# Four graph layers for 128 small graphs on one core: new instruction orders, the residual constant in two pairs, and unsplit transposed weights read out by ScalarE

## The chip, the core and the metric

The kernel runs on one core of a Trainium2 chip. It has TensorE (PE; its weight loads are a track of their own, PEld), VectorE (DVE), ScalarE (ACT), GpSimd (POOL), the queue that issues most transfers (SP) and 16 DMA engines. The metric is device time in microseconds of one launch.

## The reference, cut to what matters

```python
x = layernorm(x + gcn(x, adj) )          # h = x@W + b; adj@h / row sum of adj
x = layernorm(x + linear_att(x, adj))    # softmax over nodes of q.(adj@(k*mask)) / 16, times v
x = layernorm(x + mha(x, adj))           # 8 heads, scores * (adj + adj), softmax, Wo
x = layernorm(x + hyper(x, adj))         # D^-1 H B^-1 H^T(.)W^T + b twice, relu and layernorm between
```

x is 128 graphs x 128 nodes x 256, adj is 128 x 128 x 128, the weights are 256 x 256 to 256 x 512, all in float32. The last layer's result is y + x, and a constant part of y that depends only on the node (its count times beta@W2, plus the bias b2, halved) is added to the residual beforehand: this is the residual constant, c3.

## The kernel before

The graphs are worked on in 32 groups of G = 4. The work of a group is cut into stages, and a step is one stage of one graph (or of the whole group), such as `h1.2`. Matrix products of stages marked by six or twelve passes are made from operands split in a high and a low part (`rows3`, L516); ACT writes the high part out of PSUM and DVE the low part (`copy_out` L716, `low` L1041). Each layernorm runs DVE (statistics, L1026 and L1031), POOL (root, L884 to L889), ACT (normalise, L724).

**Who orders the work.** Nothing is scheduled at run time. Every engine walks a list of steps written out by hand, and waits on semaphores in that order. There are three lists for each engine: FIRST_TEXT (group 0's first half, and all preparation of weights), ORDER_TEXT (one round, walked 31 times: once, and then in a loop of 30), LAST_TEXT (second half of the last group). In a round, a step with + belongs to the next group, one without to the present group, so each round has the early stages (at, ax, h0, x1t, amx, xg, wt, pb, v1, x2t, q, k, mp, sc, z, exp) of one group among the late ones (pt, cx, wo, tx, h1, mn, y) of the group before. On the PE list the number behind the colon is the PSUM bank (of 8) that the step fills; pt, sc0 and sc1 take two banks from that number. A step waits until those who read the bank's earlier content are done (`early`, L471 on).

**Steps that the change and the prediction touch.**

- `c3` (POOL, `c3_`, L956 to L963): the residual constant of all four graphs in two instructions of 128x1024 (L959 multiply, L962 add). `x3b` (L969) adds it to the normalised x3 of one graph; `y` on DVE needs that.
- `wm` (POOL, L925): w times mask, 128x4; it waits for the four xg reads of DVE (L1064). `wt` (PE, L540) transposes it, then follow wmax and wnorm (DVE), wexp (ACT), and `pb` (PE, L544). In the POOL order of a round, wm stands right behind c3.0; in the PE order wt stands behind tx.1 (L610).
- `pt` (PE, L589): eight transposes of one graph's attention; `pt` on ACT (L792) copies two banks to pT in one instruction of 128x1024; `cx` (PE, L597) reads pT. cx.0 is the first PE step of a round.
- `exp0`, `exp1` (ACT, L785): four heads each, eight instructions; `mp` (PE L569, ACT L716): 128x130; `hb` (POOL, L930) is needed by mp.
- `turn` (PE, L633): the 20 transpositions of weights in FIRST. `turnhi`/`turnlo` (ACT L802, DVE L1161) read out those of v, q, k and w1 in two parts. The twelve others (mask, q and k of layer 1, the row vectors, o and w2) stay unsplit, and DVE copies them (`turn_lo`, L1158). `scale` (DVE, L1179) multiplies w2 by gamma once all of w2 is read out, `hi_w2`/`lo_w2` (ACT L817, DVE L1185) split it.
- `ACT_LOADS` (L869): ACT issues the loads of L1's Wqk (512 KB), L0's W and L1's Wv (256 KB each) before its first step. All other transfers are issued by SP (L392 to L429).

Of the kernel before, what the change touches and what calls it, by code (L numbers as in the profile page):

```python
# [17 lines left out]
P = 128  # L18
G = 4
HEADS = 8  # L20
RG = 4
# [32 lines left out]
        ln2_norm.0 ax.3+ ln0_norm.0+ v2.3 tx.0 exp0.3 ln0_norm.1+ x1t.0+ exp1.3 x1t.1+ amx.0+ ln0_norm.2+
        pt.2 x1t.2+ amx.1+ ln0_norm.3+ cx.2 amx.2+ ln2_norm.1 x1t.3+ hbc.0+ amx.3+ relu.0 pt.3 cx.3 tx.1
        wexp.0+ ln3_norm.0 ln2_norm.2 ln2_norm.3 tx.2 ln1_norm.0+ mn.0 ln1_norm.1+ relu.1 ln1_norm.2+ tx.3
        x2t.0+ ln1_norm.3+ x2t.1+ x2t.2+ x2t.3+ relu.2 relu.3 ln3_norm.1 q0.0+ k1.0+ q1.0+ ln3_norm.2 k0.0+
# [9 lines left out]
        wmax.0+ tx_lo.1 ln2_aggr.2 wnorm.0+ wo.3 ln2_stats.3 pcol.0+ ln2_aggr.3 v1.0+ v1.1+ ln1_stats.0+
        ln1_aggr.0+ v1.2+ ln1_stats.1+ ln1_stats.2+ ln1_aggr.1+ ln1_aggr.2+ v1.3+ tx_lo.2 ln1_stats.3+ h1.1
        ln1_aggr.3+ mn_lo.0 ln3_stats.1 tx_lo.3 x2t_lo.0+ x2t_lo.1+ x2t_lo.2+ x2t_lo.3+ h1.2 h1.3 ln3_aggr.1
        y.0 ln3_stats.2 ln3_stats.3 ln3_aggr.2 ln3_aggr.3 ln4_stats.0 ln4_aggr.0 mn_lo.1 z0.0+ z1.0+  # L70
        zmax0.0+ mn_lo.2 y.1 ln4_stats.1 zmax1.0+ ln4_aggr.1 z0.1+ mn_lo.3 zmax0.1+ zrcp.0+ z1.1+ y.2
# [32 lines left out]
        hT.0+ ax_lo.0+ turnlo.0+ asum.0+ turnlo.1+ hT.1+ hT.2+ hT.3+ turnlo.2+ lo_w0.0+ ax_lo.1+ turnlo.3+
        turnlo.4+ h0.0+ ln0_stats.0+ ax_lo.2+ ln0_aggr.0+ h0.1+ ln0_stats.1+ ax_lo.3+ ln0_aggr.1+ h0.2+
        ln0_stats.2+ gramlo.0+ ln0_aggr.2+ h0.3+ gramlo.1+ ln0_stats.3+ x1t_lo.0+ ln0_aggr.3+ x1t_lo.1+
        turnlo.5+ turnlo.6+ xg.0+ x1t_lo.2+ xg.1+ x1t_lo.3+ lo_wv1.0+ xg.2+ xg.3+ turnlo.7+ wmax.0+ wnorm.0+
        pcol.0+ v1.0+ ln1_stats.0+ v1.1+ ln1_aggr.0+ v1.2+ ln1_stats.1+ turnlo.8+ ln1_aggr.1+ ln1_stats.2+
# [1146 lines left out]
```

## Time and profile before

| | us |
|---|---|
| median of 3 runs (1754.32 to 1756.01) | 1755.94 |
| the profiled execution | 1754.82 |
| its span, first to last instruction | 1753.1 |
| PE busy in the span | 1725.9 |
| DVE, ACT, POOL busy | 1457.4, 1445.5, 1381.3 |
| granted TensorE clock, mean | 1.0 |

The profiled execution's own time is 1.7 us above its span. Engines' busy times are unions of the recorded instructions; matmuls overlap in the records, so for PE the distance from one start to the next says more than a duration. A row of a timeline is: start, length, engine, line, operation, output<-inputs, shapes, count, and in brackets the idle time before it with its releaser.

### The profile page before, as it was taken

How to read it: one execution, taken by the hardware profiler on the slowest of the kernel's cores; microseconds unless marked ns; L12 is line 12 of the kernel's file. 1: busy time of each engine (PE TensorE's matmuls, PEld its weight loads, DVE VectorE, ACT ScalarE, POOL GpSimd, SP SyncE). 2: the span in 40 equal slices, each digit the busy share in tenths (PEclk: the TensorE clock that was granted, in tenths of full speed). 3: DMA queues.
4: the chain of work that ended last, by engine and by line, in shares of the span. 5: the costliest groups of instructions: out<-in, count | busy, mean ns of one | idle time of the engine just before them, and what ended most of it. 6: DMA issues, size and time to landing. Idle time of an engine off the chain costs nothing. (4 is left out here: it accounts for less than half of the span.)

```text
span 1753.1 us, 52062 instructions
## 1 busy us (share of the span) xinstructions
PE 1725.9 (98%) x15358; PEld 1557.1 (89%) x15358; DVE 1457.4 (83%) x4038; ACT 1445.5 (82%) x4463; POOL 1381.3 (79%) x2825
## 2 busy tenths in 40 slices
PE   8999999999999999999999999999999999999997
PEld 6889888999889898889998998988899989989886
DVE  7988888888888888888888888888888888888886
ACT  4888888888888888888888888888888888888886
POOL 4777778787788877787877888777878778887776
PEclk9999999999999999999999999999999999999999
DMA  4111101111001111011110011110111100111000
GB/s 132 31 44 43 33 16 34 42 42 37 19 27 42 42 42 33 16 34 42 42 37 20 27 42 42 42 33 16 34 42 42 36 21 27 42 42 42 27 6 22
DMA packets 93590, 62.94 MB, mean 36 GB/s; under 512 B 8430, under 2 KB 92924, under 8 KB 93564
## 3 DMA queue, kind: packets, MB, share of 16 engines
q1 hardware_dynamic: 92748, 61.58, 11.7%
q10 hardware_dynamic: 816, 1.05, 0.2%
q8 instruction: 12, 0.20, 0.0%
q14 instruction: 14, 0.11, 0.0%
HBM read 45.82 MB, written 16.78 MB: 36 GB/s over the span
## 5 line engine op out<-in xcount | busy, mean ns | idle before, releaser
L785 ACT ACTIVATE z<-z,z_max 128x128 f32<-128x128 f32 x1024 | 399.8, 398 | 5.0 <-DVE z_max L1125 3.7
L886 POOL TENSOR_TENSOR ln_rs<-ln_ve,minus_half 128x1 f32<-128x1 f32 x640 | 352.6, 551 | 50.1
L889 POOL TENSOR_SCALAR ln_nm<-ln_mv,ln_rs 128x1 f32<-128x1 f32 x640 | 170.6, 267 | 110.1 <-POOL ln_rs L886 110.0
L884 POOL TENSOR_TENSOR ln_ve<-ln_mv,eps_col 128x1 f32<-128x1 f32 x640 | 122.7, 192 | 163.1 <-DVE ln_mv L1031 162.8
L906 POOL TENSOR_TENSOR z<-z,z_rcp 128x1024 f32<-128x1024 f32 x128 | 243.1, 1899 | 8.7 <-DVE z_rcp L1132 5.5
L516 PE MATMUL ps<-w2T,mnT 128*128 128x256 f32 x1536 | 209.0, 284 | 0.0
L516 PE MATMUL ps<-w1T,txT 128*128 128x512 f32 x768 | 204.5, 403 | 0.2 <-DVE txT L1041 0.2
L785 ACT ACTIVATION_READ_ACCUMULATOR z<-z,z_max 128x1 f32 x1024 | 200.0, 195 | 0.0
L516 PEld LDWEIGHTS ps<-w2T,mnT 128*128 128x128 f32 x1536 | 188.1, 188 | 4.2 <-DVE mnT L1041 0.4
L1041 DVE TENSOR_TENSOR mnT<-ps,mnT 128x512 fp32r<-128x512 f32 x128 | 86.7, 678 | 111.5 <-ACT mnT L716 111.5
L1125 DVE TENSOR_REDUCE z_max<-z 128x4 f32<-128x512 f32 x256 | 170.2, 675 | 0.1
L1114 DVE SCALAR_TENSOR_TENSOR z<-ps,a_hold 128x512 f32<-128x512 f32 x256 | 166.7, 682 | 0.7 <-PE ps L580 0.4
L516 PEld LDWEIGHTS ps<-w1T,txT 128*128 128x128 f32 x768 | 135.1, 189 | 22.3 <-DVE txT L1041 0.4
L724 ACT ACTIVATE h<-h,ln_nm,ln_rs 128x512 f32<-128x512 f32 x128 | 104.4, 816 | 43.9 <-POOL ln_nm L889 40.4
L621 PE MATMUL ps<-mp,h 128*128 128x128 f32 x1024 | 138.2, 278 | 0.3 <-ACT h L724 0.3
L792 ACT COPY pT<-ps 128x1024 f32<-128x1024 f32 x128 | 129.4, 1011 | 10.7 <-PE ps L589 10.7
L589 PE MATMUL ps<-ident,z 128*128 128x128 f32 x1024 | 134.8, 275 | 0.9 <-POOL z L906 0.8
L1031 DVE BATCH_NORM_AGGREGATE ln_mv<-ln_st 128x2 f32<-128x6 f32 x640 | 112.7, 176 | 27.6
L621 PEld LDWEIGHTS ps<-mp,h 128*128 128x128 f32 x1024 | 126.8, 191 | 6.6 <-ACT h L724 0.5
L516 PE MATMUL ps<-gram,x1T 128*128 128x256 f32 x768 | 126.5, 300 | 0.0
L516 PE MATMUL ps<-w,axT 128*128 128x256 f32 x768 | 126.4, 301 | 0.0
L724 ACT ACTIVATE x<-x2c,ln_nm,ln_rs 128x256 f32<-128x256 f32 x128 | 78.4, 613 | 54.0 <-POOL ln_nm L889 54.0
(154 smaller groups left out, 4912.4 us busy)
## 6 DMA issues: line engine op xcount, KB each, us to landing
x_in<-in_x_dram SPq DMA_DIRECT2D x128, 128.0 KB, 2.1
a_hold<-in_adj_dram SPq DMA_DIRECT2D x128, 128.0 KB, 2.2
out_dram<-y_out SPq DMA_DIRECT2D x128, 128.0 KB, 1.7
a_in<-in_adj_dram SPq DMA_DIRECT2D x128, 64.0 KB, 1.9
h<-in_L_gnn_W_dram SPq DMA_DIRECT2D x2, 512.0 KB, 7.1
x<-in_L_gnn_Wqk_dram ACTq DMA_DIRECT2D x1, 512.0 KB, 3.9
y_out<-in_L_gnn_W_dram ACTq DMA_DIRECT2D x1, 256.0 KB, 4.5
y_out<-in_L_gnn_Wv_dram ACTq DMA_DIRECT2D x1, 256.0 KB, 5.1
```

The source lines that it names most:

```text
L516: m = pe.matmul(o, left(i, c), right(j, c), start=(k == 0), stop=(k == len(passes) - 1))
L589: m = pe.transpose(ps[:, b + h // 4, (h % 4) * P:(h % 4 + 1) * P], z[:, g % 2, h, :], ident[:, :])
L621: m = pe.matmul(o[:, c * P:(c + 1) * P], h1[:, g, c * P:(c + 1) * P], mp[:, g, 0:P], start=True, stop=True)
L724: act.activation(dst(g), src(g), ACT.Identity, bias=nm[n][:, g:g + 1], scale=rs[n][:, g:g + 1]).then_inc(norm_made[n], 1)
L785: m = act.activation(z[:, g % 2, h, :], z[:, g % 2, h, :], ACT.Exp, bias=z_max[:, g % 2, h:h + 1], accum_out=z_sum[:, g % 2, h:h + 1])
L792: act.copy(pT[:, g % 2, :, :].rearrange("p (b h) n -> p b (h n)", b=2), ps[:, b:b + 2, :]).then_inc(read["pt"], 1)
L884: pool.tensor_tensor(ve[n][:, g:g + 1], mv[n][:, g, 1:2], (eps4_col if n == "ln4" else eps_col)[:, :], ALU.add).then_inc(eps_made[n], 1)
L886: pool.tensor_tensor(rs[n][:, g:g + 1], ve[n][:, g:g + 1], minus_half[:, :], ALU.pow).then_inc(root_made[n], 1)
L889: pool.tensor_scalar(nm[n][:, g:g + 1], mv[n][:, g, 0:1], rs[n][:, g:g + 1], -1.0, ALU.mult, ALU.mult).then_inc(shift_made[n], 1)
L906: pool.tensor_tensor(zg, zg, z_rcp[:, g % 2, :].unsqueeze(2).to_broadcast([P, HEADS, P]), ALU.mult)\
L1114: dve.scalar_tensor_tensor(out=z[:, g % 2, hs, :].rearrange("p (r c) n -> p r (c n)", r=RG // 2), in0=ps[:, b:b + RG // 2, 0:C * P], scala ...
L1125: dve.tensor_reduce(z_max[:, g % 2, hs], z[:, g % 2, hs, :], AX.X, ALU.max, negate=True)\
```

## The change

Three things: (1) c3 is made for two graphs at a time (c3.0, c3.1), with semaphore counts to match, and x3b.g waits for its pair alone. (2) The twelve unsplit transposed blocks are copied out of PSUM by ACT (`turncp`, semaphore `whole_read`) and no longer by DVE; ACT issues only the load of w0 first, then does its first step (at.0), then issues qk1 and wv1. (3) All the orders and bank numbers are new. Of the round, mp.2 and mp.3 move to the start of the next round on PE, v2.2 to the end of the round before, x2c.3 (POOL), z1.2 (DVE), and the load lh.2 (SP) move across the round's border too; sp's order is new.

```diff
 "pe":
-        cx.0:2 at.0+:4 v2.2:1 ax.0+:0 at.1+:3 at.2+:5 wo.0:7 at.3+:6 ax.1+:1 ax.2+:0 h0.0+:2 pt.1:3 h0.1+:5
-        sc1.3:6 sc0.3:1 cx.1:4 h0.2+:0 ax.3+:5 v2.3:6 tx.0:3 wo.1:2 x1t.0+:6 amx.0+:1 h0.3+:5 h1.0:0
-        x1t.1+:7 pt.2:3 amx.1+:2 xg.0+:5 x1t.2+:6 amx.2+:0 cx.2:4 xg.1+:3 amx.3+:7 x1t.3+:0 xg.2+:1 pt.3:5
-        xg.3+:4 wo.2:0 cx.3:3 tx.1:2 wt.0+:0 v1.0+:7 wo.3:3 v1.1+:6 pb.0+:5 v1.2+:4 mn.0:0 v1.3+:3 tx.2:2
-        h1.1:7 x2t.0+:6 h1.2:1 tx.3:2 x2t.1+:0 y.0:7 x2t.2+:4 x2t.3+:6 h1.3:5 q0.0+:3 k1.0+:2 q1.0+:1
-        k0.0+:5 mn.1:3 mp.0+:0 sc0.0+:1 sc1.0+:5 mn.2:7 y.1:4 mp.1+:1 mn.3:3 sc0.1+:6 sc1.1+:4 y.2:2 v2.0+:6
-        y.3:7 sc1.2+:2 sc0.2+:0 pt.0+:4 v2.1+:7 mp.2+:6 mp.3+:3
+        at.0+:4 cx.0:5 at.1+:7 mp.2:1 mp.3:2 ax.0+:0 ax.1+:3 at.2+:1 at.3+:2 wo.0:7 pt.1:4 ax.2+:1 h0.0+:0
+        sc1.3:6 sc0.3:2 cx.1:5 v2.3:0 h0.1+:6 ax.3+:1 tx.0:7 h0.2+:3 x1t.0+:0 amx.0+:6 h0.3+:1 wo.1:2 pt.2:3
+        h1.0:5 x1t.1+:7 amx.1+:0 x1t.2+:6 xg.0+:2 amx.2+:5 xg.1+:7 pt.3:1 xg.2+:4 x1t.3+:7 amx.3+:0 cx.2:5
+        cx.3:1 tx.1:6 xg.3+:2 wo.2:3 wo.3:0 wt.0+:7 h1.1:1 v1.0+:2 pb.0+:7 v1.1+:6 v1.2+:4 mn.0:0 v1.3+:2
+        tx.2:3 tx.3:6 x2t.0+:1 y.0:0 h1.2:5 x2t.1+:4 x2t.2+:3 mp.0+:7 x2t.3+:2 h1.3:0 q1.0+:2 k1.0+:1
+        k0.0+:4 q0.0+:0 mn.1:1 mp.1+:3 sc0.0+:6 sc1.0+:4 mn.2:0 v2.0+:3 sc0.1+:1 sc1.1+:6 y.1:4 mn.3:5
+        v2.1+:1 y.2:6 y.3:1 pt.0+:4 sc0.2+:2 sc1.2+:0 v2.2+:6
 "act", its last lines:
-        mn.1 ln3_norm.3 ln4_norm.0 mn.2 mp.0+ exp0.0+ mn.3 mp.1+ exp1.0+ ln4_norm.1 exp0.1+ v2.0+ exp1.1+
-        pt.0+ ln4_norm.2 ln4_norm.3
+        mn.1 ln4_norm.0 mp.1+ ln3_norm.3 mn.2 v2.0+ exp0.0+ exp1.0+ mn.3 v2.1+ exp0.1+ exp1.1+ ln4_norm.1
         pt.0+ ln4_norm.2 ln4_norm.3
 "pool":
-        xb.0+ probs.1 xb.1+ xb.2+ mask.0+ dmax.0 am.0+ xb.3+ ln2_root.0 ln0_root.0+ dinv.0 ln0_root.1+
-        probs.2 ln0_root.2+ ln2_root.1 ln0_root.3+ probs.3 c3.0 wm.0+ ln3_root.0 ln2_root.2 ln2_root.3
-        ln1_root.0+ ln1_root.1+ ln1_root.2+ ln1_root.3+ x2c.0+ x2c.1+ x3b.0 hb.0+ x3b.1 ln3_root.1 x3b.2
-        ln3_root.2 x2c.2+ ln4_root.0 ln3_root.3 x3b.3 ln4_root.1 x2c.3+ probs.0+ ln4_root.2 ln4_root.3
+        xb.0+ probs.1 xb.1+ mask.0+ xb.2+ am.0+ ln2_root.0 dmax.0 ln0_root.0+ probs.2 xb.3+ ln0_root.1+
+        ln0_root.2+ dinv.0 probs.3 ln0_root.3+ ln2_root.1 c3.0 x2c.3 x3b.0 wm.0+ hb.0+ ln3_root.0 ln2_root.2
+        ln2_root.3 ln1_root.0+ ln1_root.1+ ln1_root.2+ ln1_root.3+ c3.1 ln3_root.1 ln3_root.2 ln3_root.3
+        ln4_root.0 x2c.0+ x2c.1+ x3b.1 x2c.2+ x3b.2 x3b.3 probs.0+ ln4_root.1 ln4_root.2 ln4_root.3
 FIRST, "act", "sp" (of the new ones):
+        at.0+ at.1+ ax.0+ hi_w0.0+ at.2+ ax.1+ turncp.0+ at.3+ ax.2+ ax.3+ turncp.1+ turncp.2+ turncp.3+
...
+        turncp.18+ turnhi.7+ turncp.19+ k1.0+ q1.0+ q0.0+ v2.0+ hi_w2.0+ v2.1+ exp0.0+ exp1.0+ mp.1+ exp0.1+
+        la.0+ lx.0+ la.1+ in_b0.0+ lx.1+ la.2+ lx.2+ in_mask.0+ la.3+ lx.3+ in_k.0+ lh.0+ lh.1+ lh.2+
 LAST, "pool":
-        probs.1 dmax.0 dinv.0 probs.2 ln2_root.0 probs.3 ln2_root.1 c3.0 ln2_root.2 ln2_root.3 x3b.0
+        probs.1 dmax.0 x2c.3 dinv.0 probs.2 ln2_root.0 probs.3 ln2_root.1 c3.0 ln2_root.2 ln3_root.0
+        ln2_root.3 c3.1 ln3_root.1 ln3_root.2 ln3_root.3 x3b.0 x3b.1 x3b.2 x3b.3 ln4_root.0 ln4_root.1
...
+            def turn_whole(q, n, o):
+                act.wait_ge(made["turn"], made_order.index(("turn", n)) + 1)
+                dst = TURNS[n][1][0]
+                act.copy(dst, o[:, 0:dst.shape[1]]).then_inc(whole_read, 1)
...
-            walk(FIRST, -1)
-            act.wait_ge(read["turn"], last_turn["vec"] + 1)
+            load("w0")
+            walk({"act": FIRST["act"][:1]}, -1, FIRST)
+            load("qk1")
+            load("wv1")
+            walk({"act": FIRST["act"][1:]}, -1, FIRST)
+            act.wait_ge(whole_read, wholes.index(last_turn["vec"]) + 1)
...
             def c3_(q, g):
+                two = slice(2 * g, 2 * g + 2)
                 pool.wait_ge(dcnt_made, q + 1)
-                after(pool, x3b_made, q * G)
-                pool.tensor_tensor(c3[:, :, :], bw_all[:, :].unsqueeze(1).to_broadcast([P, G, D]),
-                                   d_cnt[:, :].unsqueeze(2).to_broadcast([P, G, D]), ALU.mult).then_inc(c3_half, 1)
-                pool.wait_ge(c3_half, q + 1)
+                after(pool, x3b_made, before(q, 2 * g + 1, G))
+                pool.tensor_tensor(c3[:, two, :], bw_all[:, :].unsqueeze(1).to_broadcast([P, 2, D]),
+                                   d_cnt[:, two].unsqueeze(2).to_broadcast([P, 2, D]), ALU.mult).then_inc(c3_half, 1)
+                pool.wait_ge(c3_half, q * PAIRS + (g + 1))
...
             def turn_lo(q, n, o):
...
-                if len(dst) == 1:
-                    dve.wait_ge(made["turn"], made_order.index(("turn", n)) + 1)
-                    dve.tensor_copy(dst[0], src).then_inc(read["turn"], 1)
```

## Rows read from the trace of the kernel before

**Rows 1.** The page: busy time, share of the span and instructions of each engine.
```profile
PE 1725.9 (98%) x15358; PEld 1557.1 (89%) x15358; DVE 1457.4 (83%) x4038; ACT 1445.5 (82%) x4463; POOL 1381.3 (79%) x2825
```

**Rows 2.** Busy time by stretch: window, length, engines busy (instructions), PEclk, DMA share, GB/s.
```profile
5.00:12.20 7.20, 6.90 (x27) 5.68 (x28) 4.43 (x13) 1.91 (x6) 4.30 (x6) 1.00 0.94 285
12.20:52.40 40.20, 35.06 (x255) 29.00 (x253) 34.20 (x87) 25.93 (x78) 19.35 (x37) 1.00 0.28 81
52.40:1713.60 1661.20, 1653.23 (x14819) 1496.45 (x14818) 1394.60 (x3877) 1390.45 (x4308) 1331.27 (x2727) 1.00 0.11 34
```

**Rows 3.** Who waited for whom, PE alone: us in total, times, longest us.
```profile
PE ps L540 <- POOL wm L925: 7.7, 29, 0.3
...
PE ps L569 <- POOL hb L930: 1.1, 1, 1.1
```

**Rows 4.** Timeline of PE in one round, from one cx.0 to the next.
```profile
856.03 0.65 PE L597 MATMUL ps<-pT,v 128*32 128x128 f32 x16
...
878.16 0.71 PE L610 MATMUL ps<-mp,x 128*128 128x128 f32 x4
879.15 0.27 PE L540 MATMUL ps<-ident,wm 128*4 128x128 f32 x1 [0.28 <-POOL wm L925]
879.17 0.96 PE L516 MATMUL ps<-wv,x1T 128*128 128x256 f32 x6
879.97 0.84 PE L516 MATMUL ps<-woT,cT 128*128 128x256 f32 x6
880.65 0.88 PE L516 MATMUL ps<-wv,x1T 128*128 128x256 f32 x6
...
887.24 0.64 PE L610 MATMUL ps<-mp,x 128*128 128x128 f32 x4
887.72 0.38 PE L554 MATMUL ps<-ident,x 128*128 128x128 f32 x2
...
908.80 0.83 PE L569 MATMUL ps<-hb,hT 128*128 128x130 f32 x4
909.61 0.64 PE L597 MATMUL ps<-pT,v 128*32 128x128 f32 x16
```

**Rows 5.** Timeline of POOL in the same round, around c3 and wm.
```profile
874.56 1.90 POOL L959 TENSOR_TENSOR c<-bw_all,d_cnt 128x1024 f32<-128x1024 f32 x1
876.53 2.40 POOL L962 TENSOR_TENSOR c<-c,b_all 128x1024 f32<-128x1024 f32 x1
878.88 0.21 POOL L925 TENSOR_TENSOR wm<-w,mask 128x4 f32<-128x4 f32 x1
```

**Rows 6.** Groups of POOL instructions by shape: busy us, mean ns of one, idle before.
```profile
L918 POOL TENSOR_TENSOR amT<-aT,mask 128x512 f32<-128x512 f32 x28 | 29.2, 1042 | 0.0
```

**Rows 7.** Timeline of ACT at the end of the same round.
```profile
900.85 0.40 ACT L785 ACTIVATE z<-z,z_max 128x128 f32<-128x128 f32 x1 [0.16 <-DVE z_max L1125]
...
902.87 0.26 ACT L716 COPY mp<-ps 128x130 f32<-128x130 f32 x1
903.03 0.41 ACT L785 ACTIVATE z<-z,z_max 128x128 f32<-128x128 f32 x1
...
908.42 1.00 ACT L792 COPY pT<-ps 128x1024 f32<-128x1024 f32 x1
```

**Rows 8.** Timeline of PE in the first group: its first sums and h0.0.
```profile
5.11 0.79 PE L501 MATMUL ps<-aT,x_in 128*128 128x128 f32 x2 [1.60 <-DMA x_in<-in_x_dram]
...
12.24 1.67 PE L516 MATMUL ps<-w,axT 128*128 128x256 f32 x12
```

**Rows 9.** Timeline of DVE towards the first group's end.
```profile
39.03 0.74 DVE L1158 COPY c<-ps 128x256 f32<-128x256 f32 x2
39.81 2.88 DVE L1179 TENSOR_SCALAR x<-c,cols 128x256 f32<-128x256 f32 x4
43.10 0.69 DVE L1114 SCALAR_TENSOR_TENSOR z<-ps,a_hold 128x512 f32<-128x512 f32 x1 [0.41 <-PE ps L580]
```

**Rows 10.** Timeline of POOL in the last group: ln2_root.2, straight behind c3.
```profile
1730.27 0.19 POOL L884 TENSOR_TENSOR ln_ve<-ln_mv,eps_col 128x1 f32<-128x1 f32 x1
```

More of the change, by code:

```diff
@@ L54 @@
[L54 to L57, printed above, removed]
-        mn.1 ln3_norm.3 ln4_norm.0 mn.2 mp.0+ exp0.0+ mn.3 mp.1+ exp1.0+ ln4_norm.1 exp0.1+ v2.0+ exp1.1+
+        at.0+ cx.0 at.1+ mp.2 mp.3 ax.0+ v2.2 at.2+ at.3+ ax.1+ exp0.2 pt.1 ax.2+ exp1.2 ln2_norm.0 cx.1
@@ L67 @@
[L67 to L71, printed above, removed]
@@ L102 @@
+        exp1.1+ pt.0+
     """,
     "dve": """
[L104 to L108, printed above, removed]
@@ new lines @@
+        ax_lo.3+ ln0_stats.1+ h0.2+ ln0_aggr.1+ ln0_stats.2+ h0.3+ ln0_aggr.2+ ln0_stats.3+ ln0_aggr.3+
+        gramlo.0+ x1t_lo.0+ hT.3+ gramlo.1+ x1t_lo.1+ xg.0+ x1t_lo.2+ x1t_lo.3+ xg.1+ ecnt.0+ xg.2+ xg.3+
+        lo_wv1.0+ wmax.0+ turnlo.6+ wnorm.0+ turnlo.7+ pcol.0+ v1.0+ ln1_stats.0+ ln1_aggr.0+ v1.1+
+        ln1_stats.1+ ln1_aggr.1+ v1.2+ ln1_stats.2+ ln1_aggr.2+ v1.3+ ln1_stats.3+ turnlo.8+ ln1_aggr.3+
+        turnlo.9+ turnlo.10+ x2t_lo.0+ turnlo.11+ x2t_lo.1+ x2t_lo.2+ x2t_lo.3+ turnlo.14+ scale.0+ scale.1+
@@ L113 @@
+        scale.2+ c2lo.0+ scale.3+ lo_wo.0+ turnlo.15+ z0.0+ zmax0.0+ z1.0+ zmax1.0+ z0.1+ zmax0.1+ z1.1+
+        zrcp.0+ zmax1.1+ bwlo.0+ lo_w2.0+ zrcp.1+ z0.2+
     """,
     "pool": """
-        xb.0+ xb.1+ mask.0+ xb.2+ am.0+ xb.3+ ln0_root.0+ ln0_root.1+ ln0_root.2+ ln0_root.3+ rep.0+ wm.0+
-        half.0+ ln1_root.0+ ln1_root.1+ ln1_root.2+ ln1_root.3+ x2c.0+ x2c.1+ rep.1+ x2c.2+ hb.0+ x2c.3+
-        probs.0+
+        xb.0+ xb.1+ xb.2+ xb.3+ mask.0+ am.0+ ln0_root.0+ ln0_root.1+ ln0_root.2+ ln0_root.3+ wm.0+ rep.0+
@@ L366, in build, with turned_out @@
         halves = [n for n, (_, dst, _) in enumerate(TURNS) if len(dst) == 2]
+        wholes = [n for n, (_, dst, _) in enumerate(TURNS) if len(dst) == 1]
+        def turned_out(n):
+            return (read["turn"], halves.index(n)) if n in halves else (whole_read, wholes.index(n))
         SPLITS = {"w0": (raw["w0"], w0), "wv1": (raw["wv1"], wv1), "wo": (woT_full, woT), "w2": (w2T_full, w2T)}
@@ L486, in early @@
                     if (other, og, away) == (SOURCE.get(stage), g, a):
+                        continue
+                    if other == "turn":
+                        semaphore, place = turned_out(og)
+                        if need(semaphore, away, place):
+                            yield
                         continue
@@ L645, in bw @@
             def bw(a, g, o):
-                need(read["turn"], a, last_turn["w2"])
+                need(whole_read, a, wholes.index(last_turn["w2"]))
                 pe.wait_ge(rep_made, rep_order.index(("rep", 1)) + 1)
@@ L810, in run @@
                     if n == "wo":
-                        act.wait_ge(read["turn"], last_turn["o"] + 1)
+                        act.wait_ge(whole_read, wholes.index(last_turn["o"]) + 1)
                     elif n == "w2":
@@ L850, in _, with walk @@
                 stages[f"hi_{n}"] = split(n)
-            def walk(orders, it):
-                bank = BANKS_OF[id(orders)]
+            def walk(orders, it, whole=None):
+                bank = BANKS_OF[id(whole or orders)]
                 for stage, g, ahead, _ in orders["act"]:
                     q = it + ahead
-                    if stage in ("turnhi", "gramhi"):
+                    if whole and stage in ("q0", "q1", "k0", "k1"):
+                        act.wait_ge(whole_read, wholes.index(last_turn["vec"]) + 1)
+                    if stage == "turncp":
+                        turn_whole(q, g, ps[:, bank["turn", g], :])
+                    elif stage in ("turnhi", "gramhi"):
                         stages[stage](q, g, ps[:, bank["turn", halves[g]] if stage == "turnhi" else bank["gram", g], :])
@@ L984, in weights @@
                 elif stage == "mask":
-                    pool.wait_ge(read["turn"], last_turn["mask"] + 1)
+                    pool.wait_ge(whole_read, wholes.index(last_turn["mask"]) + 1)
                 elif stage == "x2c":
```

118 lines of the change are left out of this document (62 added, 56 removed).

## The prediction, made before the changed kernel was run

> **What bounds the kernel now.** I read the page first. PE is busy for 98% of the span, PEld for 89%, DVE, ACT and POOL for about 80% [rows 1]. Matmuls overlap in the records, so 98% does not say how much PE could still lose; it says that the others have room, some 8 to 10 us in a round. (The Trainium skill, Perfetto Trace Analysis, Identifying the Most-Contended Engine, says the same of matmul busy time and judges by the weight loads' share. Nothing below is worked out from that.) Next, the windows: the 31 rounds take 1661.2 us of the span, and PE sits idle for only 8 us of them; the first group has 5.1 us of idle PE after h0.0 has begun, in 40.2 us [rows 2]. The chance therefore lies in the round, times 31. One round is the distance from one cx.0 to the next: 909.61 - 856.03 = 53.58 us [rows 4].
>
> The waits of PE then name one wait that comes back in nearly every round: wt waits for wm of POOL, 29 times, 7.7 us in all [rows 3]. The idle time in that view is the smaller half of it, since the sequencer's stall first eats the overlap with the matmul before. From start to start, tx.1 takes 879.15 - 878.16 = 0.99 us, while tx.3, which is also followed by a transposition, takes 887.72 - 887.24 = 0.48 us [rows 4]. So the wait costs **0.51 us a round**. Its cause is in the POOL timeline: c3 holds the queue from 874.56 for 4.33 us, and wm starts when it ends (876.53 + 2.40) [rows 5].
>
> **The round, part by part.**
>
> *c3 in pairs.* Two instructions of 128x1024 become four of 128x512. A 128x512 instruction of the same engine takes 1.04 us against 1.90 for 128x1024 [rows 5, 6], so an instruction has a fixed part of 2 x 1.04 - 1.90 = 0.18 us, and c3 costs POOL 2 x 0.18 = 0.36 us more a round. That hides: POOL has 20% of idle time in the rounds [rows 2]. Each half takes (4.33 + 0.36)/2 = 2.3 us.
>
> *wm against wt.* Before wm, POOL's new list has the same roots, xb and probs as the old, half of c3 less 2.3 for 4.3, and in addition x2c.3 and x3b.0, of 128x256, some 0.7 each (between half and the whole of the 1.04 of rows 6). It comes to wm at 878.88 - 856.03 = 22.85, less 2.0, plus 1.4, so 22.3 us into a round. wm also needs the DVE read of xg.3, which PE now does behind tx.1: I find it done at 22.6. PE would have come to wt at 22.6 without the wait (879.15 - 856.03 = 23.12, less 0.51 [rows 4]). In the new list, mp.2, mp.3 (0.81 together with the loop's branch [rows 4]) and wo.3 (0.7) are now ahead of it and v2.2 (0.8) is not: 23.3. Slack is 0.5 us or more. The 0.51 us goes. Next late there would be pb, which needs the chain wmax, wexp, wnorm: before, v1.0, wo.3 and v1.1 stood between wt and pb (0.80 and twice 0.7), now h1.1 (six passes of twice the columns, over 1.3) and v1.0 (0.8), as much.
>
> *Neighbours on PE.* A six-pass step takes 879.97 - 879.17 = 0.80 us behind an unsplit float32 step, and 880.65 - 879.97 = 0.68 behind another split one [rows 4]. Counting both lists round the loop, there are 22 changes from an unsplit to a split step before and 19 after. At most 3 x 0.12 = 0.36 us; but changes between float32 products and transpositions grow in number, which rows 4 don't price. Between 0 and 0.36 I take 0.1. The Trainium skill (TensorE: Matmul & The Clock Gate, Back-to-back issue gap) gives the spacing of load and matmul pairs by their columns alone, without a term for the neighbour. By that this term is 0 and the rounds would give 3 us less; rows 4 show that a neighbour does count.
>
> *The round's border.* This is the new order's thin place. PE's first two steps are now at.0 in bank 4 and cx.0. Both wait for ACT's copy of pt.0, at.0 because pt.0 fills banks 4 and 5, cx.0 because it reads pT. Before, ACT went from the first exp at 900.85 to the end of that copy at 909.42, and cx.0 started at 909.61 [rows 4, 7]. In the new list ACT has the same work between these two, except mp.1 (903.03 - 902.87 = 0.16 [rows 7]). On PE, three mp (0.35 to 0.4 each) leave the stretch from mn.1 to the border and one v2 (0.8) enters: 0.2 to 0.3 us less. PE thus comes to the border 0.25 earlier, the copy 0.16 earlier, and there was 0.19 between: a slack of about 0.1. Behind the copy nothing of PE can pass. The exps themselves wait for z and zmax of DVE, which follow mn.1 as before.
>
> *Other waits.* I went through both lists with the spacings of the trace and asked for each PE step when its input and its bank are free. The closest are cx.1 (0.1 us behind the copy of pt.1), y.3 (0.2), tx.0, tx.1 and y.0 (0.3). I charge 0.1 us a round for what of these slips.
>
> Round: -0.51 - 0.10 + 0.12 = -0.49; times 31 = **-15.2 us**. Bounds: -0.87 if everything fits and the neighbours give all (-27), and -0.1 if the border takes back most (-3).
>
> **The first group.** ACT issues 768 KB (Wqk, Wv) only after at.0. At the 285 GB/s of the stretch from 5.0 to 12.2 [rows 2] those are 2.7 us of traffic that no longer stand before x and adj; PE waited 1.60 us for x alone, and h0.0 started at 12.24 [rows 8]. ACT pays for it with two issues between at.0 and at.1, 1 us, which the landing of x covers in part. hb, whose root is computed earlier, no longer holds mp.0: 1.1 us [rows 3]. The twelve copies (0.74 for two, so 0.37 each [rows 9], 4.4 us) leave DVE, busy 34.2 of 40.2 us, for ACT, busy 25.9 [rows 2]. But scale must wait until ACT has read the last block of w2, and that readout now stands behind the one of k0; scale (2.88 us) and what follows it hold back the first z, which started at 43.10, right behind scale [rows 9]. So I take 2.7 + 1.1, less 0.5 for that: **-3.3 us**. Ends: -6 if the DVE copies count as well, +1 if ACT's new copies make x2T or q late. SP's new order only shifts loads of 2 to 8 us that are used later than 20 us.
>
> **The last group.** ln2_root.2 started at 1730.27, straight behind c3 of 4.3 us [rows 5, 10]; now half of c3 stands before it, so it can start 2 us earlier, and x3b no longer stands before the ln3 roots. wo.3's own chain gives only half a microsecond. **-1.5 us**, between -3 and +1.
>
> **Sum.** -15.2 - 3.3 - 1.5 = -20.0. From the profiled execution, 1754.8 - 20.0 = 1734.8; it lies 1.1 us below the median of the runs, and against the median 1755.9 it gives **1736**.
>
> **Rivals.**
> (A) As summed, 1727 to 1744: chance 0.72.
> (B) The wait moves to the border. at.0 finds pt.0 not yet copied; a round ends up at 53.4, 0.2 less than now: 31 x 0.2 + 4.8 = 11 us, 1745 (1744 to 1752). For it: slack of only 0.1, and the copy has always ended just before PE needed it [rows 4, 7]. Against: the exps are at the same distance from mn.1. 0.13.
> (C) Slower, by the same place. The copy of pt.0 comes late because v2.0 now stands before exp0.0 and z1.2 has moved into the next round, so that DVE's first steps, and with them mp.2, mp.3 and ax.0 of PE, are late in turn. Each 0.1 us over a round of 53.58 costs 3.1 us; the edges give 4.8, so it decides from 53.74 on (53.85 to be seen). At 53.9 the kernel takes 1755.9 + 9.9 - 4.8 = 1761. For it: PE would have to be held 0.9 us a round by a queue that has 8 us to spare; against: the walk found no such place. 0.09.
> (D) The change does little: wm goes earlier but xg.3's read is now the last input (its PE step was moved behind tx.1), and the wait stays at 0.4 us; with the edges 1752 to 1756. 0.06.
>
> **Numbers.** The prediction is that of A. The range 1729 to 1750 leaves out C, D and the lowest and highest ends of A and B. A measurement of this kernel tells some 0.2%, 3.5 us, from no change. Faster: 0.84 (A, B but for its end); same: 0.07; slower: 0.09.
>
> **What would show it.** In the changed profile: no idle PE before L540 (now 0.3 us in 29 rounds), tx.1 to its follower 0.36 to 0.5; a round of 53.1 between two at.0; c3 as four instructions of 1.0 to 1.3 us. A row of PE waiting for ACT pT or for v, of 0.1 us and more and 28 times or oftener, would show B. h0.0 at about 9 to 10 us, the first z at about 40 and the first round from 49. I am wrong on the mechanism if the round stays above 53.4, wrong on the edges if the first round starts after 51.5.

## The result, and the profile after

The changed kernel takes 1747.17 us (median of 5 runs, 1746.04 to 1747.42) against 1755.91 for the kernel before (5 runs, 1754.32 to 1756.01): a ratio of 0.9952, 95% interval 0.9939 to 0.9965. That is 8.7 us faster. I had said 1736, so 20 us faster. The direction and the range (1729 to 1750) hold; the size is less than half. 1745, the figure of rival B, lies nearest.

The page, busy time and share of the span of each engine, answers to [rows 1]; the three windows are the first group from 12.20 us on, the 31 rounds, and the last group, and answer to [rows 2].

```profile
PE 1727.2 (99%) x15358; PEld 1551.7 (89%) x15358; DVE 1439.1 (82%) x4026; ACT 1451.0 (83%) x4475; POOL 1387.1 (79%) x2889
...
12.20:52.40 40.20, 36.50 (x254) 30.81 (x253) 30.02 (x79) 27.94 (x89) 18.12 (x36) 0.96 0.28 85
52.81:1706.90 1654.09, 1653.71 (x14820) 1490.16 (x14820) 1381.33 (x3877) 1393.64 (x4310) 1338.46 (x2792) 1.00 0.11 34
1706.90:1745.60 38.70, 30.16 (x256) 25.22 (x256) 23.60 (x57) 25.16 (x68) 26.45 (x54) 0.99 0.06 22
```

The spans differ by 1753.1 - 1745.6 = 7.5 us. By these windows the rounds give 1661.2 - 1654.1 = 7.1 of it, the last group (1753.1 - 1713.6) - 38.7 = 0.8, and the first group takes 0.4 back (the rounds begin at 52.8 us, not 52.4). But the windows of the last group do not begin at the same step in the two kernels. The same step in both is the last group's cx.0, before and after:

```profile
1714.93 0.64 PE L597 MATMUL ps<-pT,v 128*32 128x128 f32 x16 [1.42 <-ACT v L716]
```
```profile
1707.77 0.64 PE L610 MATMUL ps<-pT,v 128*32 128x128 f32 x16
```

From there to the end it is 38.2 us before and 37.8 after, so the last group gave 0.3 us. From the first cx.0 (52.40 and 53.05 us) to this one, the rounds gave 7.8, and the first group took 0.65 back. So all of the gain is in the rounds, 0.23 us in each, where I had 0.49 (some 0.6 us came where they pass over into the last group). The 3.3 us of the first group are missing, and most of the last group's 1.5.

What I said of wt and wm came true. This is PE's timeline around tx.1 in one round, and POOL's around the constant; they answer to [rows 4] and [rows 5].

```profile
873.15 0.71 PE L623 MATMUL ps<-mp,x 128*128 128x128 f32 x4
873.62 0.95 PE L529 MATMUL ps<-gram,x1T 128*128 128x256 f32 x6
...
875.83 0.27 PE L553 MATMUL ps<-ident,wm 128*4 128x128 f32 x1
```
```profile
871.69 1.04 POOL L988 TENSOR_TENSOR c<-bw_all,d_cnt 128x512 f32<-128x512 f32 x1
872.81 1.28 POOL L991 TENSOR_TENSOR c<-c,b_all 128x512 f32<-128x512 f32 x1
...
875.45 0.20 POOL L952 TENSOR_TENSOR wm<-w,mask 128x4 f32<-128x4 f32 x1
```

tx.1 takes 873.62 - 873.15 = 0.47 us to its follower (0.99 before), wt no longer waits, and half of the constant takes 2.4 us. So the 0.5 us are gone, and half as much has come back elsewhere. PE's own waits don't say where: asked for the rounds (154 to 1640 us), that view has no row. A stall that eats only the overlap with the matmul before leaves no idle time. One has to compare the steps from start to start, or take the waits away, which the first two runs do.

### The profile page after: what moved, and what is told of

The parts are those of the page before. It is cut to its first block, busy times and chain, and to the rows that moved or that the text cites. A ratio compares the mean times of both kernels' runs of the same rounds, so it can differ in the third digit from the quotient of the medians.

```text
span 1745.6 us, 52318 instructions
## 1 busy us (share of the span) xinstructions
PE 1727.2 (99%) x15358; PEld 1551.7 (89%) x15358; DVE 1439.1 (82%) x4026; ACT 1451.0 (83%) x4475; POOL 1387.1 (79%) x2889
## 4 chain that ended last, share of the span: by engine, by line
PE 98%; ACT 1%; DVE 1%; issue 0%; DMA 0%; POOL 0%; SPq 0%; POOLq 0%; DVEq 0%
PE ps L529 58%; PE ps L634 7%; PE ps L602 6%; PE ps L593 5%; PE ps L610 4%; PE ps L514 4%; PE ps L623 4%; PE ps L545 3%; PE ps L567 2%; PE ps L540 2%; PE ps L582 2%; PE ps L518 1%; ACT z L798 1%; PE ps L646 0%; DMA x_in<-in_x_dram 0%
## 5 line engine op out<-in xcount | busy, mean ns | idle before, releaser
L529 PE MATMUL ps<-w2T,mnT 128*128 128x256 f32 x1536 | 198.0, 281 | 0.3 <-DVE mnT L1070 0.3
L529 PEld LDWEIGHTS ps<-w2T,mnT 128*128 128x128 f32 x1536 | 183.2, 188 | 4.5 <-DVE mnT L1070 0.5
L1143 DVE SCALAR_TENSOR_TENSOR z<-ps,a_hold 128x512 f32<-128x512 f32 x256 | 171.9, 682 | 10.3 <-PE ps L593 6.7
L529 PE MATMUL ps<-wvT,x2T 128*128 128x256 f32 x768 | 124.7, 298 | 0.9 <-DVE bw_all L1200 0.8
L1060 DVE BATCH_NORM_AGGREGATE ln_mv<-ln_st 128x2 f32<-128x6 f32 x640 | 105.5, 173 | 23.4
```

Source lines behind the costliest of these rows:

```text
L529: m = pe.matmul(o, left(i, c), right(j, c), start=(k == 0), stop=(k == len(passes) - 1))
L1060: dve.bn_aggr(mv[n][:, g, :], st[n][:, g, :]).then_inc(aggr_made[n], 1)
L1143: dve.scalar_tensor_tensor(out=z[:, g % 2, hs, :].rearrange("p (r c) n -> p r (c n)", r=RG // 2), in0=ps[:, b:b + RG // 2, 0:C * P], scala ...
```

## The experiments

Each run is beside runs of the kernel before on the same chip, and its ratio is to them. Their medians lie between 1754.2 and 1755.9 us, depending on the chip, so 1 or 2 us between kernels of different sets are not yet a difference. "Round" is the mean distance from one first step to the next, and a step's place in the round is the median over the loop's rounds, both worked out from the timelines of one profiled execution. That has a spread too: the changed kernel's round is 53.36 us in one profile and 53.43 in the other (after_again), so rounds that differ by less than 0.1 are not told apart.

### TensorE's order by itself

The weights and inputs are constants, the other engines do nothing but fill them in, and TensorE walks ORDER 31 times (all values are therefore other ones; first and last group are left out). It waits only for its own steps on the same bank:

```diff
-                    if not any(s in begun for s in later) and need(read[other], away, None if other in per_group else og):
-                        yield
+                    if passed.get(other, -1000) < count:
...
+                        pe.wait_ge(made[other], group["now"] * len(row) + count)
+                        yield
```

> TensorE walks the old round order 31 times; nothing else runs, its operands are constants, and its steps wait only for its own earlier steps on the same bank, so the text of the round's other engines is left out. The traced round of before was 53.59 us, of which 0.51 was the wt wait and about 0.3 loop branch and refill, so every theory expects 52.7 to 53.1 us a round. The number that decides is the difference to the new order, next run.

> The same with the new round order. Theory N (the neighbours of the tiled score and context steps, by which I took 0.10 us off, came out the other way): the new order alone costs 0.15 to 0.3 us more a round than the old order alone. Theory W (the order itself is worth what I forecast, and the +0.26 us a round that is missing are new small waits for ScalarE at the border and in front of the transposes): the new order alone costs 0 to 0.15 us less than the old one.

From one cx.0 to the next, TensorE's timeline of the old order alone and, in the second fence, of the new order alone:

```profile
253.19 0.64 PE L527 MATMUL ps<-pT,v 128*32 128x128 f32 x16
...
305.94 0.64 PE L527 MATMUL ps<-pT,v 128*32 128x128 f32 x16
```
```profile
253.28 0.64 PE L535 MATMUL ps<-pT,v 128*32 128x128 f32 x16
...
305.69 0.65 PE L535 MATMUL ps<-pT,v 128*32 128x128 f32 x16
```

The old round alone takes 52.75 us, the new one 52.41 (whole kernels, one run each: 1679.4 and 1670.2 us). Theory N is refuted: the new order is cheaper by **0.34 us**, by more than either theory had, near the upper bound (0.36) that I had given for the neighbours and three times the 0.10 I took. The split steps account for it: together they take 33.20 us of the old round and 32.80 of the new one, 0.40 less with three fewer changes from an unsplit to a split step, and all other steps 0.06 more. Set beside the rounds in the kernels, this gives the ledger:

| us a round | before | after |
|---|---|---|
| TensorE's order alone | 52.75 | 52.41 |
| tx.1 held up for wt | 0.42 | 0 |
| border: from mp.2 and mp.3 (old), at.0 (new) to ax.0, ax.1, wo.0 | 0.33 | 0.57 |
| all else, in pieces of 0.03 to 0.11 | 0.09 | 0.38 |
| round in the kernel | 53.59 | 53.36 |

The order and the wt wait together should have given 0.76. New small waits took 0.53 of it: 0.24 at the border and 0.29 elsewhere. The largest of these are in front of x2t.0 and y.0 (0.17 together), at.0 (0.08), and tx.1 and the pair x1t.2, xg.0 (0.05 each).

### The constant in pairs, alone

> The kernel before, with the residual constant in two pairs and nothing else changed: every order of TensorE, ScalarE and VectorE stays. Theory 1 (the wt wait of 0.51 us hangs on the 4.7 us that GpSimd spends on the constant in one piece, and the rest of the old order has nothing late behind it): the wait goes, the round is 53.1 us, total 1740 (1738 to 1742), that is faster than the whole change at 1747. Theory 2 (the old order was balanced on this wait, and what stood behind it is late next: pb, v1, x2t): 0.1 to 0.4 us of it come back a round, total 1744 to 1753.

```diff
-        ln1_root.3+ x2c.0+ x2c.1+ x3b.0 hb.0+ x3b.1 ln3_root.1
+        ln1_root.3+ c3.1 x2c.0+ x2c.1+ x3b.0 hb.0+ x3b.1 ln3_root.1
```

Measured: 1802.6 us, ratio 1.0271 (1.0257 to 1.0285), 47 us **slower**. Both theories missed. The wt wait did go (tx.1 takes 0.55), and in its place PE has two larger ones in every round. PE's waits in the rounds, then ScalarE's timeline and GpSimd's in one round:

```profile
PE ps L581 <- ACT kT L750: 24.4, 27, 0.9
PE ps L517 <- ACT qT L750: 18.6, 27, 0.7
```
```profile
918.39 0.82 ACT L725 ACTIVATE h<-h,ln_nm,ln_rs 128x512 f32<-128x512 f32 x1 [2.92 <-POOL ln_nm L890]
919.11 0.66 ACT L750 ACTIVATE qT<-ps,cols 128x512 f32<-128x512 f32 x1
```
```profile
910.93 1.04 POOL L962 TENSOR_TENSOR c<-bw_all,d_cnt 128x512 f32<-128x512 f32 x1
912.05 1.29 POOL L965 TENSOR_TENSOR c<-c,b_all 128x512 f32<-128x512 f32 x1
...
917.11 0.18 POOL L885 TENSOR_TENSOR ln_ve<-ln_mv,eps_col 128x1 f32<-128x1 f32 x1
```

c3.1 occupies GpSimd from 910.93 for 2.4 us, ln3_root.1 comes behind it, and ln3_norm.1 stands ahead of the reads of q and k in ScalarE's list. So the first q is read 1.7 us later in the round (40.1 instead of 38.4 us behind cx.0). PE then waits for a bank that q still holds, and for k, and a round takes 55.09. In the next kernel the pair stands where the old order leaves GpSimd idle.

> The kernel before with the constant in two pairs, as in c3_pairs_only, but the second pair and the two x3b adds that need it stand behind ln3_root.3 on GpSimd, where the old order left 3.6 us idle. Theory P (place: what cost 1.5 us a round there was ln3_root.1 held back 1.7 us by the pair ahead of it, and through it ln3_norm.1 and ScalarE's reads of q and k; the pair itself is free): the wt wait goes and nothing comes in its place, round 53.1 to 53.2, total 1739 to 1744. Theory S (the split itself, two more instructions and a fuller GpSimd, is what costs): over 1756.

```diff
-        ln1_root.3+ c3.1 x2c.0+
+        ln1_root.3+ x2c.0+
...
-        x3b.1 ln3_root.1 x3b.2 ln3_root.2 x2c.2+ ln4_root.0 ln3_root.3 x3b.3 ln4_root.1
+        x3b.1 ln3_root.1 ln3_root.2 x2c.2+ ln4_root.0 ln3_root.3 c3.1 x3b.2 x3b.3 ln4_root.1
```

Measured: 1744.3 us, ratio 0.9943 (0.9929 to 0.9956), round 53.18, no wait of PE in the rounds. Theory P holds. With this one move and every other order old, the kernel is 2.9 us below the median of the whole change. The same kernel was run once more, beside others.

> c3_pairs_late once more, beside the other two: 1743.5 to 1745, if it really is better than the whole change.

Measured: 1743.9 us (1742.9 to 1744.6), 0.9937 (0.9924 to 0.9951); the changed kernel's two sets of runs lie at 1746.0 to 1747.4 and 1745.9 to 1748.9, with no overlap. By the ratios, which take the chip out, the lead is smaller (0.9943 and 0.9937 against 0.9952 and 0.9949, some 2 us) and the intervals overlap. Either way, the rest of the change adds nothing to this one move.

> The changed kernel with the residual constant in one piece again, at the place of its first pair; all orders stay. wm is 2.4 us later on GpSimd. Theory 1 (the wt wait is the price of the whole constant): TensorE waits 0.5 to 2 us a round in front of wt, total 1763 to 1810. Rival (the new order took wt far enough back to cover it): 1747 to 1752.

Measured: 1810.7 us, 1.0322 (1.0308 to 1.0336), just above the top of what theory 1 expected. PE's waits in the rounds name wm, as in [rows 3] but six times larger:

```profile
PE ps L553 <- POOL wm L952: 45.4, 27, 1.7
```

The new order lives by the pairs: wm now has x2c.3 and x3b.0 ahead of it.

### Relief at the border

The border is the stretch of the ledger that ends with wo.0. The next three edits each aim at one wait there.

> The changed kernel with one word moved: in VectorE's round order cx_lo.0 stands ahead of hT.1. Theory B (border: of the 0.95 us by which the new round runs over its order alone, some 0.2 is wo.0 waiting for the low half of cT, which VectorE writes from 2.43 to 2.85 us although ScalarE's half was there at 1.87): wo.0 starts 0.2 us earlier, total 1740 to 1742. Rival (wo.0 starts at 2.99 us for another reason, or hT.1 0.4 us later makes mp late, or the time is made up at the next wait): 1746 to 1748.

```diff
-        z1.2 asum.0+ hT.0+ hT.1+ cx_lo.0 zmax0.2
+        z1.2 asum.0+ hT.0+ cx_lo.0 hT.1+ zmax0.2
```

Measured: 1746.7 us, 0.9957 (0.9943 to 0.9970), less than 1 us below the changed kernel: the rival. wo.0 did start 0.21 us earlier, and nothing was left of it at x1t.2.

> The changed kernel with ScalarE's ln4_norm.3 carried over the border: it stands behind the reads of mp.3 in the next round instead of ahead of the read of at.0, so that read no longer waits for GpSimd's ln4_root.3. Theory B (the border is what the new order's 0.34 us of cheaper TensorE work is lost to: ScalarE is 0.9 us late with at.0 there): ax.0, ax.1 and wo.0 start up to 0.3 us earlier, round 53.05 to 53.2, total 1738 to 1743. Rival (what is gained at the border is waited for again before x1t and tx, as in after_cxlo_first): 1745 to 1748.

```diff
 "act":
-        at.0+ cx.0 at.1+ mp.2 mp.3 ax.0+ v2.2
+        at.0+ cx.0 at.1+ mp.2 mp.3 ln4_norm.3- ax.0+ v2.2
...
-        pt.0+ ln4_norm.2 ln4_norm.3
+        pt.0+ ln4_norm.2
```

(A minus marks a step of the group before. Round 1 is written out, so that its wait is on a constant.) Measured: 1747.4 us, 0.9952 (0.9939 to 0.9966): again the rival. The same edit on c3_pairs_late follows.

> c3_pairs_late with the same carried ln4_norm.3. The old border has only 0.07 us in front of ax.0 to give: both theories expect 0 to 3 us less than c3_pairs_late, 1741 to 1745; if the carried step delays the reads behind it, 1745 to 1748.

Measured: 1759.8 us, 1.0026 (1.0017 to 1.0035): 15 us slower than without the edit, and 12 above the highest time that I had expected. PE stalls 0.5 us between at.2 and wo.0 in every round (step 0.55 against 0.06). By the lists, wo.0 fills bank 7, and v2.1, which has it before, is read by ScalarE right behind the carried norm. That would be the delayed read that the expectation had named, at a much higher price; that this bank is the cause was not tested.

In after_norm_carried DVE and ACT show where the gained time is waited for again. VectorE's timeline, ScalarE's and GpSimd's, 8 to 10 us into one round:

```profile
863.33 0.43 DVE L1058 BATCH_NORM_STATS2 ln_st<-xb 128x6 f32<-128x256 f32 x1
864.01 0.42 DVE L1073 TENSOR_TENSOR axT<-ps,axT 128x256 fp32r<-128x256 f32 x1 [0.26 <-ACT axT L729]
```
```profile
863.12 0.60 ACT L737 ACTIVATE x<-xb,ln_nm,ln_rs 128x256 f32<-128x256 f32 x1 [0.35 <-POOL ln_nm L919]
863.63 0.35 ACT L729 CAST axT<-ps 128x256 fp32r<-128x256 f32 x1
```
```profile
861.60 0.25 POOL L972 TENSOR_SCALAR d_pos<-d_sum 128x4 f32<-128x4 f32 x1
861.81 0.19 POOL L914 TENSOR_TENSOR ln_ve<-ln_mv,eps_col 128x1 f32<-128x1 f32 x1
862.08 0.57 POOL L916 TENSOR_TENSOR ln_rs<-ln_ve,minus_half 128x1 f32<-128x1 f32 x1
```

VectorE's ax_lo.3 waits for ScalarE's read of ax.3; that stands behind ln0_norm.0, which waits 0.35 us for GpSimd's ln0_root.0; and ln0_root.0 waits for nobody (no bracket): it starts when d_pos ends. GpSimd is simply busy. Looking back from there in the changed kernel, GpSimd's waits from the start of that stretch (847.5) to 861.5 are:

```profile
POOL z L933 <- DVE z_rcp L1161: 3.3, 1, 3.3
POOL ln_nm L916 <- POOL ln_rs L913: 0.9, 5, 0.2
POOL xb L923 <- issue: 0.3, 1, 0.3
POOL d_max L966 <- POOL d_sum L962: 0.2, 1, 0.2
```

The 3.3 us lie right before probs.0, which starts at 847.47. From there, over the border and up to ln0_root.0 at 860.30, GpSimd waits only for itself and for the branch, for 13 us; behind it come probs.2, xb.3 and ln0_root.1 with gaps of 0.1 us. The new order has one root more in this stretch (ln4_root.1, which stood ahead of probs.0). And it is not only this stretch. GpSimd's waits in the whole round, from 852.36 to 905.72:

```profile
POOL ln_nm L916 <- POOL ln_rs L913: 3.5, 20, 0.2
POOL z L933 <- DVE z_rcp L1161: 3.3, 1, 3.3
POOL ln_ve L911 <- DVE ln_mv L1060: 0.9, 1, 0.9
POOL xb L923 <- issue: 0.3, 1, 0.3
```

It waits for another engine twice, 4.2 us in all; the other wait of that size is for its own root, 0.17 us in each layernorm, which no other step fills. So the page's 79% busy does not mean that 21% of the round is free: it is 8%, most of it in one place.

### Taking GpSimd's load out of that stretch

> The changed kernel with ln4_root.3 on GpSimd and ln4_norm.3 on ScalarE both carried over the border to where the next round has idle time (behind ln3_root.1 and behind the read of k1). GpSimd has 1.2 us less and ScalarE 0.6 us less to do between the scores and the first norms of the next round. Theory G (that full stretch of GpSimd, through ln0_root.0 and ln0_root.2 and ScalarE's norms, holds amx.1 and x1t.2, and so eats the new order's gain): ln0_norm.2 and x1t.2 come 0.2 to 0.5 us earlier, total 1732 to 1741. Rival (the stretch is held by TensorE's own work or by VectorE): 1744 to 1748; if the carried steps disturb q and k where they now stand: over 1748.

```diff
 "pool":
-        c3.1 ln3_root.1 ln3_root.2
+        c3.1 ln3_root.1 ln4_root.3- ln3_root.2
...
-        probs.0+ ln4_root.1 ln4_root.2 ln4_root.3
+        probs.0+ ln4_root.1 ln4_root.2
 "act":
-        mp.0+ k1.0+ ln3_norm.2
+        mp.0+ k1.0+ ln4_norm.3- ln3_norm.2
...
-        pt.0+ ln4_norm.2 ln4_norm.3
+        pt.0+ ln4_norm.2
```

Measured: **1731.7 us** (4 runs, 1731.2 to 1735.0), ratio 0.9874 (0.9859 to 0.9889). That is 15.5 us below the changed kernel and just past the fast end of what theory G expected. Its rounds, and GpSimd's ln0_root.0 in one of them, which now waits for its input:

```profile
52.80:1691.00 1638.20, 1637.43 (x14820) 1488.42 (x14819) 1379.44 (x3877) 1392.12 (x4310) 1337.42 (x2792) 1.00 0.11 34
```
```profile
852.12 0.19 POOL L914 TENSOR_TENSOR ln_ve<-ln_mv,eps_col 128x1 f32<-128x1 f32 x1 [0.15 <-DVE ln_mv L1065]
```

> The changed kernel with ScalarE's ln4_norm.3 carried to behind the read of k1 in the next round, exactly as in after_root_carried, but GpSimd's ln4_root.3 left at the end of the round. Theory G (GpSimd's full stretch is the cause): the border gains as in after_norm_carried and x1t.2 gives it back, total 1745 to 1748. Rival (ScalarE's full stretch is the cause): 1731 to 1738, as after_root_carried.

Measured: 1749.2 us (6 runs), 0.9968 (0.9956 to 0.9980). Relief of ScalarE alone gives nothing, or costs 2 us. This kernel and after_root_carried differ only in where GpSimd does ln4_root.3, and that one place is worth 17.5 us, 0.60 us a round. Where the steps stand in the round (us):

| | wo.0, PE | ln0_root.0, POOL | ax_lo.3, DVE | ln0_root.2, POOL | x1t.2, PE | round |
|---|---|---|---|---|---|---|
| changed kernel | 2.99 | 7.93 | 10.13 | 13.26 | 15.29 | 53.36 |
| after_cxlo_first | 2.78 | 7.96 | 10.17 | 13.30 | 15.34 | 53.47 |
| after_norm_carried | 2.61 | 7.95 | 10.16 | 13.29 | 15.32 | 53.43 |
| after_norm_far | 2.61 | 7.95 | 10.16 | 13.29 | 15.32 | 53.42 |
| after_root_carried | 2.61 | 7.35 | 9.60 | 12.72 | 14.88 | 52.82 |

(The profiled executions of after_cxlo_first and after_norm_carried took 1750.6 and 1750.5 us, 3 to 4 above their medians, so their rounds are not longer than the changed kernel's by more than that spread.) Three kernels bring wo.0 forward and leave ln0_root.0 where it was; x1t.2 then doesn't move. The one that brings ln0_root.0 forward moves all of it. It moves by 0.6 us and not by the 1.2 us of the carried root, because it now waits for VectorE.

### The first group

> The changed kernel with mp.0 of the first group behind x2t.1 on TensorE and behind x2t.0 on ScalarE. Theory C (TensorE's idle stretch from 28.5 to 30.9 us, which ends in the wait for ScalarE's norm behind the read of mp.0, is what the fall of its granted clock to 0.50 from 31.5 to 34.5 us follows): x2t.0 starts 0.3 to 1 us earlier, the clock stays at 1.00, the first group is 1.5 to 2.5 us shorter, total 1744.5 to 1746. Rival (the clock's fall is chance of one execution, and idle time there is made up before the round): the same as the changed kernel, 1746 to 1748.

```diff
 "pe", FIRST:
-        turn.13+:6 mp.0+:4 x2t.0+:6 x2t.1+:0 turn.14+:1
+        turn.13+:6 x2t.0+:6 x2t.1+:0 mp.0+:4 turn.14+:1
```

Measured: 1747.4 us, 0.9959 (0.9946 to 0.9973). The rival: in its profile the clock fell all the same (0.50 from 33.1 to 36.5 us), and its first k comes no earlier. The changed kernel once more:

> The changed kernel once more, beside the next three on the same chip, and for a second look at its first group. All theories: 1746 to 1748. In the five profiles with the new first group so far, TensorE's granted clock fell to 0.50 near 32 us in two and stayed at 1.00 in three, with the same idle stretch ahead of it; if that is chance, either can show here, and the round starts about 1.4 us earlier where it stays.

Measured: 1746.9 us, 0.9949 (0.9936 to 0.9963); the clock stayed at 1.00. The new round behind the old first group:

> The new round, last group and paired constant behind the first group of the kernel before (all three loads up front, VectorE reads the unsplit weights out, its tail fitted to the new round). Theory F (the new first group gains under 1 us: from 12.2 us on TensorE had no gap until 24 us anyway, and the earlier h0 only trades places with transposes): total 1746 to 1749. Rival (the new first group is worth the 3.3 us that I forecast, hidden by the round): 1749.5 to 1752.

Measured: 1748.0 us, 0.9957 (0.9943 to 0.9971). Theory F: the old first group is worse by 1.0 us, within the runs' spread (and in its profile, an execution of 1749.0 us, the granted clock was at 0.50 for 3.4 us of the first round). The other way round, the new first group ahead of the old round, with the pair in its bad and in its good place:

> As the run before, but with the first group of the changed kernel (weights read out by ScalarE, two loads later, its orders; its tail is fitted to the old round). Since the first group gained nothing in the trace (round from 52.8 against 52.4), both theories expect the time of the run before within 2 us. If the fall of TensorE's clock to 0.50 near 32 us is a matter of that group alone, it shows here too.

Measured: 1808.6 us, 1.0307 (1.0292 to 1.0321), 6 us over c3_pairs_only, where at most 2 were expected.

> c3_pairs_late with the first group of the changed kernel (tail fitted). Theory F (the new first group gains under 1 us): 1743 to 1745. Rival (its 2.7 us earlier h0.0 counts): 1740 to 1742.

Measured: 1747.1 us, 0.9959 (0.9946 to 0.9973). Both theories missed: here the new first group costs 3 us. The profiled executions differ by 4.2: 0.4 in the first group, 2.3 in the rounds (53.25 against 53.17 us each), and 1.5 in the last group, where the granted clock fell to 0.50 for 6.8 us in the slower one. The rounds' part is no larger than between two executions of the changed kernel; whether and why a first group should change them stays open.

TensorE's first 24 us before, and in the second profile of the changed kernel (after_again), there with the stretch of 28 to 32 us:

```profile
0.00:12.20 12.20, 7.35 (x28) 5.87 (x29) 5.05 (x20) 3.46 (x8) 4.99 (x12) 1.00 0.80 248
12.20:24.00 11.80, 11.80 (x85) 10.62 (x84) 9.31 (x32) 7.26 (x19) 4.66 (x15) 1.00 0.78 230
```
```profile
0.00:12.20 12.20, 6.79 (x26) 5.37 (x27) 3.71 (x12) 3.69 (x10) 2.83 (x9) 1.00 0.76 238
12.20:24.00 11.80, 11.80 (x84) 10.52 (x83) 10.06 (x34) 8.02 (x24) 6.03 (x16) 1.00 0.89 261
28.00:32.00 4.00, 2.23 (x16) 1.56 (x15) 3.67 (x12) 2.46 (x8) 2.97 (x10) 1.00 0.00 0
```

h0.0 starts at 9.50 in the changed kernel (12.24 in [rows 8]), as forecast. But TensorE had filled the wait for the loads with weight transpositions: it did 7.35 us of work in the first 12.2 us before, and 6.79 now, and from 12.2 to 24.0 it has no gap in either (0.3 us in the first profile of the changed kernel). The earlier h0 changed places with work that has to be done anyway.

## Why the prediction was right or wrong

The sum was -20.0: -15.2 for the rounds, -3.3 and -1.5 for the first and last group. The spans gave -7.8, +0.65 and -0.3. By the signs that I had set, the edges are wrong (the first round starts at 52.8 us, after 51.5), and the round, 53.36, is just under the 53.4 that would have refuted the mechanism.

- **The wt wait, -0.51 us a round: right.** 0.41 to 0.50, by the mechanism named (0.41 is c3_pairs_late's round against the old one, 53.18 and 53.59, and 0.42 is tx.1 against the order alone); wm comes at 23.1 us of the round instead of the 22.3 I had, still in time.
- **c3's price: right** (2.4 us for a half, 2.3 said).
- **Neighbours, -0.10: mis-sized.** 0.34 measured for the order alone. I had the bound (0.36) and chose the low end because float32 products next to transpositions could have cost something; all unsplit steps together cost 0.06 more.
- **Border and slipped waits, +0.12 (0.02 for the border, 0.1 for the rest): the step that failed.** They cost 0.53 us a round, 0.41 more than I had, which is 12.7 us over 31 rounds; the neighbours' surplus made up for some 7 of it. For the border I counted what ScalarE does between the exps and the copy of pt.0, and found 0.1 us of slack. That much is nearly true: at.0 starts 0.06 us behind the end of that copy. But I asked of each PE step only when its own input and bank are free, with the other engines' steps at the distances of the old trace. I did not add up GpSimd's new list from probs.0 over the border to ln0_root.1. It has no idle place in it, so that whatever TensorE gains at the border comes back as a wait 12 us later. after_root_carried shows the size: with ln4_root.3 and its norm out of that stretch, the round is 52.82, and the 0.95 us over the order alone shrink to 0.41. I had also counted GpSimd's idle 20% as free to hide work in, and called it a queue with 8 us to spare; 3.5 us of that are the roots' waits for themselves, and what it has for others is 4.2. Rows for it were there: POOL's place for every step could be worked out as I did for wm.
- **Rival B** named the place, the border, and came nearest in time, which is in good part luck. Its mechanism, the wait for pt.0, is only 0.08 us of it (v2.2 to at.0 takes 0.90, and 0.82 in the order alone); the two relief runs show that the border's waits are worth nothing by themselves.
- **The first group, -3.3: failed.** The 2.7 us at h0.0 came true, but I counted them as if TensorE were idle before it. hb's 1.1 us was replaced by a wait of 1.2 us for ScalarE's norm in front of x2t.0. In 8 profiles with the new first group and round (one of them after_mp_late) the first cx.0 starts at 51.6 to 53.9 us, in 5 with the old ones at 52.3 to 52.8.
- **The last group, -1.5: a fifth**, 0.3 measured. ln2_root.2 did start 1.5 us earlier (13.8 us behind the last group's cx.0, 15.3 before), but the last of the roots, ln4_root.3, came only 0.3 earlier (33.8 against 34.1).

The Trainium skill (Perfetto Trace Analysis, Identifying the Most-Contended Engine) takes the engine of highest occupancy as the one to work on. Here that is TensorE, and its time was the kernel's, but what held it up was GpSimd, with the lowest occupancy of the four, 79%: moving one 1.2 us step of its list, with the norm that follows it, gave 15.5 us. What fits is the page's other remark (Optimization Strategy), that the contended engine can change over time.

## What to carry to other kernels

When steps are reordered, add up every engine's new list between its last real idle place and the next step that the critical engine waits for. An engine that is 80% busy on average can have all its free time in one or two places of the round (here 4.2 us of 53.4), and gains ahead of the end of a full stretch are given back there. A stall removed in a round that is cyclic is worth only what the next full stretch lets through; what an order itself is worth can be measured by walking it alone, without waits. And where a wait for loads is already filled with other work of the same engine, as here, earlier loads gain nothing.
